# The V product of a graph layer by Strassen's algorithm, with the score bias as a column of V, on one core

## The reference, cut to what matters

```
h  = relu(layernorm(x))                          # x: 256 x 512
q, k, v = h Wq^T + bq, h Wk^T + bk, h Wv^T + bv  # each 256 x 512
w  = adj * exp(q k^T)                            # adj, w: 256 x 256
x1 = x + (w / rowsum(w)) v
h1 = relu(layernorm(x1))
A  = adj + I ;  d = rowsum(A) ^ -0.5
y  = x1 + (A * d * d^T) (h1 W + b)               # the output
```

## Time and profile before

| what | value |
|---|---|
| time, median of 3 runs | 1684.84 us (1682.74 to 1685.69) |
| the profiled execution | 1685.13 us, span of its instructions 1683.3 us |
| granted TensorE clock, mean | 0.996 |
| TensorE matmul busy | 1657.5 us, 98% |
| VectorE busy | 1369.1 us, 81% |
| ScalarE busy | 757.2 us, 45% |
| GpSimd busy | 555.8 us, 33% |
| DMA | 212.63 MB, mean 126 GB/s, the queue of SyncE 50.0% of 16 engines |

### The profile page before, as it was taken

How to read it: one execution, slowest core, us unless ns; L and a number is a source line. 1 busy time by engine, 2 the same in 40 slices (tenths; PEclk the granted TensorE clock), 3 DMA queues, 4 the chain that set the end, 5 groups by cost and what they waited for, 6 DMA issues and landing times.

```text
span 1683.3 us, 33110 instructions
## 1 busy us (share of the span) xinstructions
PE 1657.5 (98%) x10828; PEld 1506.2 (89%) x10828; DVE 1369.1 (81%) x3285; ACT 757.2 (45%) x1546; POOL 555.8 (33%) x586
## 2 busy tenths in 40 slices
...
GB/s 177 120 117 146 117 126 146 107 136 143 104 143 140 103 145 139 96 154 133 102 152 128 110 147 125 118 146 119 124 146 110 133 144 103 142 139 102 147 93 29
DMA packets 494413, 212.63 MB, mean 126 GB/s; under 512 B 402496, under 2 KB 427072, under 8 KB 494400
## 3 DMA queue, kind: packets, MB, share of 16 engines
q1 hardware_dynamic: 492480, 210.89, 50.0%
...
HBM read 146.28 MB, written 66.13 MB: 126 GB/s over the span
## 4 chain that ended last, share of the span: by engine, by line
PE 97%; DVE 1%; DMA 1%; ACT 0%; issue 0%; POOL 0%; ACTq 0%; POOLq 0%; DVEq 0%; SPq 0%
PE ps L638 32%; PE ps L639 32%; PE ps L640 32%; PE ps L648 1%; DMA late<-in_L_gnn_Wq_w_dram 0%; DMA x_in<-in_x_dram 0%; DVE w_in L458 0%; DVE w_lo L451 0%; ACT wvt_hi L321 0%; DVE st_x L471 0%; ACT w_hi L323 0%; ACT late L347 0%; ACT h_hi L349 0%; POOL rs_x L298 0%; POOL hat_hi L270 0%
## 5 line engine op out<-in xcount | busy, mean ns | idle before, releaser
L347 ACT ACTIVATE late<-late,nb,sc 128x512 f32<-128x512 f32 x128 | 103.6, 809 | 509.2 <-DVE nb L542 509.2
L270 POOL TENSOR_TENSOR hat_hi<-adjt,eye 128x512 fp32r<-128x512 f32 x64 | 82.6, 1291 | 629.4 <-DVE ht_lo L610 617.3
L638 PE MATMUL ps<-ht_hi,m_hi 128*128 128x256 f32 x1024 | 287.4, 281 | 0.8 <-DVE wvt_lo L448 0.8
L639 PE MATMUL ps<-ht_lo,m_hi 128*128 128x256 f32 x1024 | 288.0, 281 | 0.0
L640 PE MATMUL ps<-ht_hi,m_lo 128*128 128x256 f32 x1024 | 287.5, 281 | 0.0
L291 POOL TENSOR_TENSOR xb<-xb,bv_row 128x512 f32<-128x512 f32 x128 | 164.8, 1309 | 256.0 <-DMA xb<-in_x_dram 256.0
L638 PE MATMUL ps<-w_hi,z_hi 128*128 128x512 f32 x512 | 202.7, 396 | 1.6 <-DVE z_lo L575 1.5
L639 PE MATMUL ps<-w_lo,z_hi 128*128 128x512 f32 x512 | 202.6, 396 | 0.0
L640 PE MATMUL ps<-w_hi,z_lo 128*128 128x512 f32 x512 | 202.3, 395 | 0.0
L638 PE MATMUL ps<-wvt_hi,ht_hi 128*128 128x512 f32 x512 | 202.2, 395 | 0.0
L640 PE MATMUL ps<-wvt_hi,ht_lo 128*128 128x512 f32 x512 | 202.1, 395 | 0.0
...
## 6 DMA issues: line engine op xcount, KB each, us to landing
...
out_dram<-late SPq DMA_DIRECT2D x128, 256.0 KB, 2.1
...
adj_in<-in_adj_dram SPq DMA_DIRECT2D x64, 256.0 KB, 2.9
adj_blocks<-in_adj_dram SPq DMA_DIRECT2D x256, 64.0 KB, 2.5
...
```

What stands on the lines that cost most here:

```text
L270: pool.tensor_tensor(hat_hi[:], adjt[:], eye[:], ALU.add).then_inc(hat_hi_ready, 1)
L347: act.activation(h1[:, t, :], x1[:, t, :], ACT.Relu, scale=sc_1[:, t:t + 1], bias=nb_1[:, t:t + 1])
L638: pe.matmul(dst, a_hi[:, c, cols], b_hi[:, c, :], start=(c == 0), stop=False)
L639: pe.matmul(dst, a_hi[:, c, cols], b_lo[:, c, :], start=False, stop=False)
```

## The change

**V by Strassen's algorithm** (Winograd's form, with seven products). h (256 x 512) and Wv^T (512 x 512) are cut in 2 x 2 blocks: of h^T the upper and lower half of the features and of the nodes, of Wv^T the halves of both its sides. V is made of seven products of half size, V1 to V7, where the plain product has eight:

- The sums of blocks of Wv^T (T1 to T4) are made once, in the prologue, and held with three of the blocks in `wt`, `wt_hi`, `wt_lo`: seven blocks, each of 256 columns and two more.
- The sums of blocks of h^T (S1 to S4, in `ht_sum`) are made by GpSimd in each step, four additions or subtractions of 128 x 256; ScalarE makes their high parts, two instructions of 128 x 512, and GpSimd their low parts, two of 128 x 512.
- TensorE computes V1, V6, V5, V4, V2, V7, V3 in this order, six matmuls each, of 258 columns (V1, V6, V4, V2) or 256. V2 is added to V1, V7 to V6 and V3 to V5 in the same bank of PSUM. They lie in banks 4 to 7.
- ScalarE copies V1 (`v_p1`) and V5 (`v_p5`) out of PSUM. VectorE adds: `v_u2` = V1 + V6 and `v_u3` = V1 + V6 + V7, then the three quarters of V that lie in `v`; the fourth is V1 + V2 in PSUM. The low parts are three instructions in place of two.

**The score bias** h c + bb is column 256 of the blocks; `vk` takes it from `v_u3` and PSUM, one column each. The 512-column reductions `score_bias` go. `vk` is now of the same step as V.

**Order.** In VectorE's step the low part of G is split: its first half goes ahead of h1_lo, its second behind v_u2. The lower half of v_lo stands behind x1b. In GpSimd's step the sums of h^T and their low parts stand at the end, behind rs_x, and wait for V3 of the same step and for both transposes of h. In ScalarE's step the first half of g_hi stands ahead of h1. TensorE waits for x1 inside V (ahead of V5, whose bank was O's), no longer ahead of O. The load of `h_blocks` waits for the same transposes as before; only their semaphore's count now begins with graph 1.

**Prologue.** The load of Wv follows those of Wk and of the first x in SyncE's queue, ahead of adj's; TensorE begins with 12 matmuls on ones (`warm_up`); the last quarter of M stands behind the transposes of h and half of those of Wv; the first h^T is copied to SBUF by VectorE. The low part of W moves from step 0 to step 1.

The core of the diff:

```diff
-        G, Z, HT, V, O1 = 0, 2, 2, 4, 4
+        G, Z, HT, O1 = 0, 2, 2, 4
         O = (6, 2)
+        VA, VB, VC, VD = 4, 5, 6, 7
...
+        B11, T3, B21, B22, T1, T2, T4 = range(7)
+        S1, S2, S3, S4 = range(4)
+        V1, V2, V3, V4, V5, V6, V7 = range(7)
...
-                        sp.wait_ge(ht_ready[1], this - 2)
+                        sp.wait_ge(ht_ready[1], this)
...
+            def ht_sums(this):
+
+                a11, a12, a21, a22 = (ht[:, 2 * i:2 * i + 2, t * P:(t + 1) * P] for t in range(NT) for i in range(2))
+                pool.wait_ge(ht_ready[0], this)
+                pool.wait_ge(ht_ready[1], this)
+                pool.tensor_tensor(ht_sum[:, S1], a21, a22, ALU.add).then_inc(ht_sum_ready, 1)
+                pool.tensor_tensor(ht_sum[:, S3], a11, a21, ALU.subtract).then_inc(ht_sum_ready, 1)
+                pool.wait_ge(ht_sum_ready, 4 * this - 3)
+                pool.tensor_tensor(ht_sum[:, S2], ht_sum[:, S1], a11, ALU.subtract).then_inc(ht_sum_ready, 1)
+                pool.wait_ge(ht_sum_ready, 4 * this - 1)
+                pool.tensor_tensor(ht_sum[:, S4], a12, ht_sum[:, S2], ALU.subtract).then_inc(ht_sum_ready, 1)
+
+            def ht_sums_low(this):
+                pool.wait_ge(ht_sum_ready, 4 * this)
+                for k in range(2):
+                    pair = slice(2 * k, 2 * k + 2)
+                    pool.wait_ge(ht_sum_hi_ready, 2 * this - 1 + k)
+                    pool.tensor_tensor(ht_sum_lo[:, pair], ht_sum[:, pair], ht_sum_hi[:, pair].bitcast(fp32),
+                                       ALU.subtract).then_inc(ht_sum_lo_ready, 1)
...
+                if main and ahead:
+                    pool.wait_ge(v_done[V3], this)
+                    ht_sums(this + 1)
+                    ht_sums_low(this + 1)
...
+            def ht_sums_high(this):
+                for k in range(2):
+                    pair = slice(2 * k, 2 * k + 2)
+                    act.wait_ge(ht_sum_ready, 4 * this - 1 + k)
+                    act.activation(ht_sum_hi[:, pair], ht_sum[:, pair], ACT.Copy).then_inc(ht_sum_hi_ready, 1)
...
                     layer_norm_x(this, prev, older)
+                if main:
+                    if not prev:
+                        act.wait_ge(u_ready, 1)
+                    g_high(0, this)
...
-                        last.then_inc(g_hi_ready[j], 1)
-                if main:
-                    value_high(0, this)
...
+                    keep_p1(this)
+                    g_high(1, this)
+                    keep_p5(this)
...
+                    act.wait_ge(v21_ready, this)
...
+                    act.activation(v_hi[:, 1, :, 0:HD], v[:, 1, :, 0:HD], ACT.Copy).then_inc(v_hi_ready[2], 1)
...
-            def score_bias(this):
-
-                for t in range(NT):
-                    dve.wait_ge(h_ready[t], this)
-                    dve.tensor_tensor_reduce(out=unused_h[:, t, :], in0=h[:, t, :], in1=c_row[:], scale=1.0,
-                                             scalar=bb_col[:, 0:1], op0=ALU.mult, op1=ALU.add,
-                                             accum_out=vk[:, t:t + 1]).then_inc(vk_ready[t], 1)
...
+            def value_u2(this):
+
+                dve.wait_ge(v_done[V6], this)
+                dve.wait_ge(v_p1_ready, this)
+                dve.tensor_tensor(v_u2[:], ps[:, VB, 0:HD + 2], v_p1[:], ALU.add).then_inc(v_u2_ready, 1)
...
+            def value_u3(this):
...
+                dve.wait_ge(v_done[V7], this)
+                dve.tensor_tensor(v_u3[:], ps[:, VB, 0:HD + 2], v_p1[:], ALU.add).then_inc(v_u3_ready, 1)
+
+            def value_sums(this):
+                dve.wait_ge(v_done[V4], this)
+                dve.wait_ge(v_u3_ready, this)
+                dve.tensor_tensor(v[:, 1, 0, 0:HD], ps[:, VD, 0:HD], v_u3[:, 0:HD], ALU.add).then_inc(v21_ready, 1)
+                dve.scalar_tensor_tensor(vk[:, 1:2], ps[:, VD, HD:HD + 1], bb_col[:, 0:1], v_u3[:, HD:HD + 1],
+                                         ALU.add, ALU.add).then_inc(vk_ready[1], 1)
+                dve.wait_ge(v_done[V3], this)
+                dve.wait_ge(v_u2_ready, this)
+                dve.tensor_tensor(v[:, 0, 1, 0:HD], ps[:, VC, 0:HD], v_u2[:, 0:HD], ALU.add).then_inc(v12_ready, 1)
+                dve.wait_ge(v_p5_ready, this)
+                dve.tensor_tensor(v[:, 1, 1, 0:HD], v_u3[:, 0:HD], v_p5[:], ALU.add).then_inc(v22_ready, 1)
+
+            def value_low(this):
+                dve.wait_ge(v_hi_ready[0], this)
+                dve.tensor_tensor(v_lo[:, 0, 0, 0:HD], ps[:, VA, 0:HD], v_hi[:, 0, 0, 0:HD].bitcast(fp32),
+                                  ALU.subtract).then_inc(v_lo_ready[0], 1)
...
+                dve.wait_ge(v_hi_ready[1], this)
+                dve.tensor_tensor(v_lo[:, 0, 1, 0:HD], v[:, 0, 1, 0:HD], v_hi[:, 0, 1, 0:HD].bitcast(fp32),
+                                  ALU.subtract).then_inc(v_lo_ready[1], 1)
+
+            def value_low_lower(this):
+                dve.wait_ge(v_hi_ready[2], this)
+                dve.tensor_tensor(v_lo[:, 1, :, 0:HD], v[:, 1, :, 0:HD], v_hi[:, 1, :, 0:HD].bitcast(fp32),
+                                  ALU.subtract).then_inc(v_lo_ready[2], 1)
...
+                    if main:
+                        g_low(0, this)
                     for t in range(NT):
                         dve.wait_ge(h1_ready[t], this - 1)
                         dve.tensor_tensor(h1_lo[:, t, :], h1[:, t, :], h1_hi[:, t, :].bitcast(fp32),
                                           ALU.subtract).then_inc(h1_lo_ready[t], 1)
...
+                if main:
+                    value_u2(this)
+                    g_low(1, this)
...
+                    if second:
+                        statistics(this + 2, lambda: value_u3(this), lambda: value_sums(this))
...
+                    value_low_lower(this)
...
                     last.then_inc(s_sum_ready, 1)
                     dve.wait_ge(s_sum_ready, this)
                     dve.tensor_tensor(sd[:], s_sum[:], dn[:], ALU.mult).then_inc(sd_ready, 1)
-                if main and ahead:
...
+                if main and prev:
...
+                    p_low(this)
...
+            def value(k, bank, left, cols, block, width, first=True):
+
+
+                product(ps[:, bank, 0:width], 2, left, cols,
+                        (wt_hi[:, block, :, 0:width], wt_lo[:, block, :, 0:width]), first).then_inc(v_done[k], 1)
...
+                upper, lower, whole = slice(0, P), slice(P, 2 * P), slice(0, P)
+                if prev and older:
+                    pe.wait_ge(y_ready[0], this - 2)
+                    pe.wait_ge(y_ready[1], this - 2)
+                weights_ready(8)
+                value(V1, VA, ht_rows(0), upper, B11, HD + 2)
+                pe.wait_ge(ht_sum_lo_ready, 2 * this)
+                value(V6, VB, sums(S2), whole, T2, HD + 2)
+                if prev:
+                    pe.wait_ge(x1_ready[0], this - 1)
+                value(V5, VC, sums(S1), whole, T1, HD)
+                value(V4, VD, ht_rows(1), lower, T4, HD + 2)
+                pe.wait_ge(v_p1_ready, this)
+                value(V2, VA, ht_rows(1), upper, B21, HD + 2, first=False)
+                pe.wait_ge(v_u2_ready, this)
+                value(V7, VB, sums(S3), whole, T3, HD, first=False)
+                pe.wait_ge(v_p5_ready, this)
+                value(V3, VC, sums(S4), whole, B22, HD, first=False)
...
-                    for t in range(NT):
-                        if prev and older:
-                            pe.wait_ge(y_ready[t], this - 2)
-                        cols = slice(t * P, (t + 1) * P)
-                        product(ps[:, V + t, :], DC,
-                                (ht_hi, ht_lo), cols, (wvt_hi, wvt_lo)).then_inc(v_done[t], 1)
+                    values(this, prev, older)
...
+                    warm_up()
+                    m_product(range(DC - 1))
+                    pe.wait_ge(ident_ready, 1)
+                    transpose_ht(this + 1)
+                    pe.wait_ge(wv_loaded, 16)
+                    transpose_wv(range(2))
+                    m_product(range(DC - 1, DC))
+                    pe.wait_ge(ht_ready[0], this + 1)
+                    pe.wait_ge(ht_ready[1], this + 1)
+                    transpose_wv(range(2, DC))
+                    pe.wait_ge(wvt_kept[0], 2)
+                    bias_products()
...
-                            pe.wait_ge(v_lo_ready[t], this)
+                            pe.wait_ge(*((vk_ready[0], this) if t == 0 else (v_u3_ready, this)))
...
-                    pe.wait_ge(v_lo_ready[1], this)
-                    if prev:
-                        pe.wait_ge(x1_ready[0], this - 1)
+                    for part in v_lo_ready:
+                        pe.wait_ge(part, this)
+                    pe.wait_ge(v12_ready, this)
+                    pe.wait_ge(v21_ready, this)
+                    pe.wait_ge(vk_ready[1], this)
```

(44 more changed lines are left out.)

266 lines of the change are left out of this document (164 added, 102 removed).

## The result

The changed kernel takes 1775.13 us (median of 4 runs, 1769.79 to 1779.49) against 1685.2 us before: ratio 1.0535, 95% interval 1.0504 to 1.0566. It is slower by 90 us, where +56 was forecast, and the time lies 3 us above the range (1772). The profiled execution took 1769.8 us, span 1768.0.

The account below looks back on a forecast made before the run. TensorE bounded the kernel before (25.46 us a step); VectorE would become the bound at 24.0 + 2.4 = 26.4 us. 62 steps add 58 us and the start takes 2: 1685.1 + 58 - 2 = 1741 us, range 1654 to 1772.

Parts of the forecast that it names:

- TensorE: V's matmuls on TensorE take 5.01 us in place of 5.59; were TensorE still the bound, a step takes 24.88 us.
- VectorE's work without holds: VectorE's step: 22.7 us of work after net +0.64, 24.0 us with small PSUM extras and the waits that stay.
- The 22.0 us "taken" before: VectorE's old step of 25.46 us less its 3.44 us of waits over 0.3 us each.
- The holds: VectorE waiting for the port beside GpSimd at x1b, v_lo's lower half, ht_lo and ve_x: 2.4 us a step (0 to 4.2).
- rs_1 about 1 us later: On GpSimd, hat follows the sums' low parts, so rs_1 comes about 1 us later than before, at the loop's edge.
- The sum: VectorE's step 24.0 + 2.4 = 26.4 us; 62 steps give +58 us, start -2, so 1741 us.
- rival 3: Transfers close a longer loop: y, h's store, h_blocks late, transposes wait; step 27.1, 1785 us; chance 0.05.
- The 1.29 us taken for a GpSimd addition of 512 columns: Pace for GpSimd's work, used for xb's two additions, a low part beside ht_lo, and the 0.74 us sums.
- Start: Prologue: first G 3 to 5 us sooner than 29.83, but V waits for Wv's blocks; -2 us, between -6 and +4.
- Rival 1: Port waits fit into VectorE's room, TensorE stays the bound; step about 24.95, 1651 us; chance 0.22.
- Rival 2: The port is not shared by scalar_tensor_tensor, so x1b passes; step 25.5, 1685 us (1660 to 1715); chance 0.17.
- the signs named ahead: In the later profile: PE idle before O1 for z_lo, stretched VectorE instructions; against: step under 25.2 us, PE waiting inside V.

Follow-up runs that it names:

- e7: Changed kernel; sums' low parts after ht_lo, hat_lo behind dn, ScalarE copies d, y's stores behind x_in, S3 first: 1652.97 us.
- e5: Changed kernel with GpSimd's sums of hT and their high and low parts made 2 or 4 columns wide, values wrong: 1662.64 us.
- e8: Changed kernel with only SyncE reordered, the stores of y issued behind x_in of the next step: 1751.32 us.
- e11: e7 without the wait for ht_lo, so GpSimd's low parts of the sums start beside ht_lo: 1652.41 us.
- e4: Changed kernel in which GpSimd makes rs_x ahead of the two additions to xb instead of behind them: 1830.51 us.

## Why the prediction was wrong

- **TensorE** was right: V in 5.01 us was forecast, 5.04 measured in e7; the step 24.88, measured 24.82.
- **VectorE's work without holds** (24.0 us with the fixed waits) was too high by about 0.6. The mean step of 26.82, less the holds (3.2, below) and what is new in the waits for rs_1 and rs_x (0.24, below), is 23.4. The 22.0 us "taken" before were not all work: VectorE was busy for 21.2 us of that step, so about 0.8 us were waits under 0.3 us each, some of which are gone. And where VectorE runs without a wait, the next instruction starts about 0.08 us ahead of the recorded end of the one before (801.95 against 800.78 + 1.24), which is gained wherever a wait of before is gone. How the 0.6 divides between the two was not tried.
- **The holds**, the step that failed, were forecast at 2.4 us and are 3.2, from the group means: ht_lo 2 x (1210 - 685) = 1.05 (taken: 1.0), x1b 2 x (1106 - 743) = 0.73 (0.6), v_lo's lower half 1207 - 683 = 0.52 (0.4), ve_x 634 - 349 = 0.29 (0.4), and two that stood nowhere: d, 659 - 169 = 0.49, and v22 (`v<-v_u,v_p`), 0.1. For d the mistake was to follow GpSimd's new work only to its own end: behind it hat runs later against VectorE, and hat had been free only because of where it stood.
- **GpSimd's queue.** "rs_1 about 1 us later" did not come: rs_1 starts 0.08 us after ve_1 as before (815.38 against 815.14 + 0.17), because the held d makes ve_1 late as well, and GpSimd even waits for it (0.46 us in this step). VectorE's wait for rs_1 did grow, from 9.9 / 64 = 0.15 us a step to 17.0 / 64 = 0.27; but it is 17.2 in all in e5, with GpSimd's sums narrow, so the sums ahead of it are not the cause, and the cause stays open. That rs_x stands behind a late xb was put at nothing: 16.8 / 64 = 0.26 us in the mean, 0.13 before, and up to 1.84 (in that long step PE then waits 2.27 us for z_lo). e8 puts the price of the transfers at 24 us.
- **The sum**: holds 0.8 and waits 0.24 too low, VectorE's work 0.6 too high, net +0.4 us a step. 60 steps x 0.42 = 25 us of the 29 by which the profiled execution (1769.8) missed 1741; the rest is mostly the start. That the time came within 3 us of the range is in part luck: with VectorE's own work right and the rest as it stood, the forecast would have been 0.6 us a step, 37 us, lower still. The range ended at 1772, with rival 3 (1785) left out above it, though the unpriced queue pointed that way.
- **Readings.** The 1.29 us taken for a GpSimd addition of 512 columns is that of hat_hi in the earlier trace rows; the earlier trace rows has 1309 ns for xb, holds included. It changes nothing above.
- **Start.** The first G came at 27.04 in place of 29.83, 2.8 us sooner, where 3 to 5 were forecast. V then waits 1.80 us for wt_lo and 2.09 for v_p1, and O 1.06. The time less 60 mean steps is 160.6 us (1769.8 - 60 x 26.82) against 157.5 before (1685.1 - 60 x 25.46): +3, not -2.
- **Rival 1** (room enough) fell for this change; with the two queues and d reordered, e11 shows the same holds of x1b and ht_lo fitting into the room. **Rival 2** (scalar_tensor_tensor is free) fell by x1b and by nb_x in e4. **Rival 3** had the right place for the uneven steps (transfers), but through xb and rs_x, not through h_blocks.
- By the Trainium skill (SBUF — State Buffer, "Who interferes with whom"), a VectorE instruction with two SBUF inputs contends with a GpSimd instruction that reads SBUF. The traces agree for scalar_tensor_tensor as well: x1b takes 736 ns alone (e5), 1106 beside GpSimd.
- Of the signs named ahead, ht_lo, x1b and v_lo stretched, ve_x's mean above 0.5 us and no wait for O came as written. PE's waits inside V, named there as proof against, came beside those for z_lo. Why v_p1 is late in so many steps (ScalarE has h1 ahead of it) was not tried apart.
